# The gate of an attention block worked out before the attention: alpha on the softmax output, one minus alpha on the recurrence's queries

## The reference

```
n = layernorm(x);  q, k, v = split(n @ Wqkv + b)
y_soft = softmax(q k^T / 4 + causal mask) @ v
state_t = retention * state_(t-1) + Gamma * (v_t outer k_t / 4);  y_stp_t = (W_static + state_t) @ q_t
alpha = sigmoid(gelu(n @ gate_w1 + gate_b1) @ gate_w2 + gate_b2)      one value per row and head
x = x + (alpha * y_soft + (1 - alpha) * y_stp) @ out_w + out_b
x = x + ffn(layernorm(x))       matmul in fp8, one scale from the largest |value| of all rows
```

## Time and profile before

| what | value |
|---|---|
| median of 3 runs | 1819.63 us (1816.71 to 1822.33) |
| the profiled execution | 1821.89 us, span 1820.2 us |
| PE, DVE, ACT, POOL busy over the span | 91%, 84%, 76%, 65% |
| mean granted TensorE clock | 0.944 |
| DMA, mean | 90 GB/s |

### The profile page before, as it was taken

The page is one execution under the profiler, slowest core; times in us unless marked ns, Lnnn a source line. Parts: engine busy times, 40 slices in busy tenths (PEclk is TensorE's granted clock), DMA queues, the critical chain, the costliest instruction groups (busy, mean ns, idle before and its releaser), DMA issues. The chain is left out here.

```text
span 1820.2 us, 44569 instructions
## 1 busy us (share of the span) xinstructions
PE 1653.8 (91%) x17464; PEld 597.0 (33%) x17464; DVE 1521.2 (84%) x1717; ACT 1391.2 (76%) x2835; POOL 1187.7 (65%) x1138
## 2 busy tenths in 40 slices
PE   4898589999999999999999999999999999996745
PEld 2553113332333333323333333333333233332632
DVE  3556889999989999998899999989999999811777
ACT  1453158889888888898888988998889989985333
POOL 1100568777777777787777777877788889840720
PEclk9898569999999999999999999999999999998865
DMA  2685441223122422231224232321243121101602
GB/s 80 216 259 168 114 101 62 85 64 99 59 68 84 111 65 82 68 95 59 71 82 111 66 87 73 87 78 63 85 117 89 50 94 48 57 10 50 230 19 81
DMA packets 115345, 163.19 MB, mean 90 GB/s; under 512 B 30081, under 2 KB 57793, under 8 KB 115137
## 3 DMA queue, kind: packets, MB, share of 16 engines
q1 hardware_dynamic: 112608, 158.74, 29.6%
q10 hardware_dynamic: 2528, 1.64, 0.3%
HBM read 121.87 MB, written 38.01 MB: 88 GB/s over the span
## 5 line engine op out<-in xcount | busy, mean ns | idle before, releaser
L1420 DVE TENSOR_REDUCE pmax<-PS 128x2 f32<-128x1024 f32 (+2 forms) x1120 | 1204.4, 1129 | 87.3 <-PE PS L1221 66.1
L1373 ACT ACTIVATE probs<-PS 128x512 f32<-128x512 f32 (+3 forms) x2304 | 1150.8, 573 | 165.0 <-PE PS L1259 82.9
L1284 PE MATMUL PS<-probs,V_g 128*17 128x256 f32 (+3 forms) x5064 | 398.5, 387 | 11.1 <-ACT o_t L1394 10.7
L1129 POOL TENSOR_TENSOR v_exp<-v_exp,k_rows 128x512 f32<-128x512 f32 x256 | 321.6, 1283 | 24.9 <-DMA v_exp<-qkv_t 24.7
L1259 PE MATMUL PS<-Q_st,K_st 50*128 50x512 f16 (+3 forms) x1408 | 287.4, 366 | 7.6 <-ACT probs L1373 6.5
L1171 POOL TENSOR_TENSOR state<-odd,q_rows 128x514 f32<-128x514 f32 x256 | 281.8, 1132 | 6.1
L1221 PE MATMUL PS<-K_st,Q_st 48*128 48x512 f16 (+3 forms) x1408 | 272.7, 357 | 0.2
L1284 PE MATMUL PS<-probs,V_first 128*17 128x256 f32 (+2 forms) x3296 | 265.5, 394 | 2.2 <-ACT o_t L1394 2.2
L1259 PE MATMUL PS<-Q_st,K_first 50*128 50x512 f16 (+3 forms) x896 | 194.3, 380 | 11.4 <-ACT probs L1373 5.4
L1221 PE MATMUL PS<-K_first,Q_st 48*128 48x512 f16 (+1 forms) x832 | 179.2, 393 | 18.8 <-DVE pmax L1420 18.5
L1160 POOL COPY carry<-odd 128x4 f32<-128x4 f32 x64 | 12.0, 187 | 259.7 <-DVE odd L1455 259.7
(11 more groups left out here) (170 smaller groups left out, 1475.1 us busy)
## 6 DMA issues: line engine op xcount, KB each, us to landing
v_exp<-qkv_t SPq DMA_DIRECT2D x256, 256.0 KB
qkv_t<-proj SPq DMA_DIRECT2D x24, 512.0 KB, 3.8
qk_parts<-parts SPq DMA_DIRECT2D x16, 512.0 KB, 5.3
Q_st<-qk_parts SPq DMA_DIRECT2D x192, 32.0 KB, 3.7
v_rows<-vaug SPq DMA_DIRECT2D x8, 544.0 KB, 6.1
xin<-x SPq DMA_DIRECT2D x8, 512.0 KB, 6.3
k_rows<-qkv_t SPq DMA_DIRECT2D x16, 256.0 KB, 4.1
q_rows<-qkv_t SPq DMA_DIRECT2D x16, 256.0 KB, 6.1
```

What stands on the lines that cost most here:

```text
L1129: pool.tensor_tensor(v_exp[:, n % RING], v_exp[:, n % RING], k_rows[:, b % 2], ALU.mult)\
L1284: mm = pe.matmul(PS[h * VW:h * VW + VN, O_BANK, first:end], v[:, kt, h * VN:(h + 1) * VN], probs[:, tile % P_SLOTS, h, first - r * P:end - ...
L1373: act.activation(probs[:, tile % P_SLOTS, h, 0:CH - r * P], PS[:, step[5], 0:CH - r * P], ACT.Exp, scale=SCORE_SCALE).then_inc(exp_done, 1)
L1420: dve.tensor_reduce(pmax[:, s % 2, pair * TPC + j:GH * TPC:PAIRS * TPC, blk], PS[:, bank:bank + SIDES, 0:width], AX.X, ALU.max).then_inc(m ...
```

## The change

alpha is worked out at the end of the prologue, in place in `z`: POOL adds the bias and, after ACT's exp, the one; DVE takes the reciprocal between two row maxima (`GATE_AT` = 16 pairs taken). PE turns it to heads on partitions, ACT makes beta = 1 - alpha from that, and SP stores it (`beta_t`, 16 heads by 4096 rows). In the attention `out_norm` multiplies the reciprocal of the sums by alpha (one more DVE instruction, 128x16), and `load_kq` loads beta too, each head's row onto its 16 partitions; POOL multiplies `q_rows` by it ahead of `lag_products_of`. All of the recurrence's output is linear in q, so what is stored is (1 - alpha) y_stp. The last block turns the softmax to channels and adds the two there; it has no rows-to-channels copy, no alpha and one DVE instruction of 128x1024 in the place of four of 128x512. The gate's logits are made for rows in their natural order now.

```
@@ prologue, SP
+                    sp.wait_ge(beta_made, 1)
+                    for n in range(TPC):
+                        sp.dma_start(beta_t[:, n * (T // TPC):(n + 1) * (T // TPC)].rearrange("h (a p) -> a h p", p=P),
+                                     beta[:, n, :]).then_inc(beta_stored, 16)
@@ prologue, POOL, at its end
+                    pool.wait_ge(z_evac, NCH + 1)
+                    pool.tensor_tensor(z[:, :, :], z[:, :, :], b2_sb[:, :].unsqueeze(1).broadcast_to([P, NT, H]), ALU.add)\
+                        .then_inc(logits_biased, 1)
+                    pool.wait_ge(gate_exp, 1)
+                    pool.tensor_tensor(z[:, :, :], z[:, :, :], ones[:, 0:1].unsqueeze(1).broadcast_to([P, NT, H]), ALU.add)\
+                        .then_inc(gate_sum, 1)
@@ prologue, PE turn_back
-                            mm = pe.matmul(PS[:, PROJ_BANK + 1, j * H:(j + 1) * H], gate_t[:, par, slice(j // 2 * PAIR + j % 2, (j // 2 + 1) * PAIR, 2)],
+                            mm = pe.matmul(PS[:, PROJ_BANK + 1, j * H:(j + 1) * H], gate_t[:, par, j * P:(j + 1) * P],
@@ prologue, PE, between the last first_maxima
+                        if pairs_made == GATE_AT + 2:
+                            pe.wait_ge(gate_ready, 1)
...
+                                mm = pe.transpose(PS[:, PROJ_BANK, n * P:(n + 1) * P],
...
+                            mm.then_inc(gate_turned, 1)
@@ prologue, ACT, at its end
+                    act.wait_ge(logits_biased, 1)
+                    act.activation(z[:, :, :], z[:, :, :], ACT.Exp, scale=-1.0).then_inc(gate_exp, 1)
+                    act.wait_ge(gate_turned, 1)
+                    act.activation(beta[:, :, :].rearrange("p n t -> p (n t)"), PS[:, PROJ_BANK, :], ACT.Identity,
+                                   bias=ones[:, 0:1], scale=-1.0).then_inc(beta_made, 1)
@@ prologue, DVE, between the last first_maxima
+                        if pairs_taken == GATE_AT:
+                            dve.wait_ge(gate_sum, 1)
+                            dve.reciprocal(z[:, :, :], z[:, :, :]).then_inc(gate_ready, 1)
@@ attention, SP load_kq, between the loads of q_rows and v_chan
+                        sp.dma_start(beta_rows[:, :], beta_t[half * HPH:(half + 1) * HPH, cols].unsqueeze(1)
+                                     .broadcast_to([HPH, HD, CH])).then_inc(beta_loaded, 16)
@@ attention, POOL lag_products_of (kq is now the first half of beta_rows)
+                        pool.wait_ge(beta_loaded, (g * N_SWEEPS + b + 1) * 16)
+                        pool.tensor_tensor(q_rows[:, b % 2, 1:1 + CH], q_rows[:, b % 2, 1:1 + CH], beta_rows[:, :], ALU.mult)\
+                            .then_inc(q_weighed, 1)
+                        pool.wait_ge(q_weighed, g * N_SWEEPS + b + 1)
@@ attention, DVE out_norm, between reciprocal and product
+                                dve.tensor_tensor(rden[:, s % 2], rden[:, s % 2],
+                                                  z[:, TPC * ORDER[s]:TPC * (ORDER[s] + 1), g * GH:(g + 1) * GH], ALU.mult)\
+                                    .then_inc(denom_gated, 1)
+                                dve.wait_ge(denom_gated, g * NCH + s + 1)
@@ last block, SP (waits soft_turned for soft, y_added for stp)
-                            sp.dma_start(stp[:, par], y_stp_t[:, :, bass.ds(it * (2 * CH) + par * CH + PAD, CH)]
-                                         .rearrange("f p t -> p f t")).then_inc(soft_loaded[par], 16)
+                            for half in range(HALF):
+                                sp.dma_start(stp[:, par, half, :],
+                                             y_stp_t[half, :, bass.ds(it * (2 * CH) + par * CH + PAD, CH)]
+                                             .rearrange("(i h) t -> h i t", h=HPH)).then_inc(stp_loaded[par], 16)
@@ last block: the stages of the first pipeline
-                    pipeline(pool, (1, residual), (0, weigh), (2, power))
+                    pipeline(pool, (0, residual), (1, power))
-                    pipeline(pe, (0, turn_stp), (2, project), (1, turn_y))
+                    pipeline(pe, (0, turn_soft), (1, project))
-                    pipeline(act, (1, columns), (2, normalise))
+                    pipeline(act, (0, normalise))
-                    pipeline(dve, (1, merge), (0, difference), (2, add_attention), (3, largest))
+                    def add_recurrence(it, par):
+                        dve.wait_ge(soft_turned, it * 2 + par + 3)
+                        dve.wait_ge(stp_loaded[par], it * 32 + 32)
+                        dve.wait_ge(attn_ready, it * 2 + par + 1)
+                        dve.tensor_tensor(y_t[:, par], PS[:, 2 * par:2 * par + 2, :], stp[:, par], ALU.add).then_inc(y_added, 1)
+                    pipeline(dve, (0, add_recurrence), (1, add_attention), (2, largest))
```

More of the change, by code:

```diff
@@ L476, in preln_attention_ffn_kernel @@
             ones = sb("ones", [P, 2], where=pro)
+            beta = sb("beta", [P, TPC, P], where=pro)
             bounds = sb("bounds", [P, 4], where=pro)
@@ L977, in preln_attention_ffn_kernel @@
             v_chan = sb("v_chan", [P, CH], where=att)
+            beta_rows = sb("beta_rows", [P, CH], where=att)
             v_exp = sb("v_exp", [P, RING, CH], where=att)
@@ L1292, in lag @@
                         pe.wait_ge(lag_products, g * N_SWEEPS + b + 1)
-                        pe.matmul(PS[:, bank, 0:PAIR], lag_sum[:, b % HALF, :], kq[:, :], start=True, stop=True)\
+                        pe.matmul(PS[:, bank, 0:PAIR], lag_sum[:, b % HALF, :], beta_rows[:, 0:PAIR], start=True, stop=True)\
                             .then_inc(lag_ready, 1)
@@ L1473, in preln_attention_ffn_kernel @@
             xn2 = sb("xn2", [P, NT, D], where=fin)
-            alpha = sb("alpha", [P, NT, H], where=fin)
             soft = sb("soft", [P, 2, TPC, D], where=fin)
@@ L1478, in preln_attention_ffn_kernel @@
             xb = sb("xb", [P, 2, TPC, D], where=fin)
-            diff = sb("diff", [P, 2, TPC, D], where=fin)
-            y = sb("y", [P, 2, TPC, D], where=fin)
             y_t = sb("y_t", [P, 2, HALF, CH], where=fin)
@@ L1585, in _ @@
                 def _(pe):
-                    def turn_stp(it, par):
-                        pe.wait_ge(soft_loaded[par], it * LOADS_PER_CHUNK + LOADS_PER_CHUNK)
-                        pe.wait_ge(y_made, it * 2 + par + 1)
-                        for half in range(HALF):
-                            for j in range(TPC):
-                                mm = pe.transpose(PS[:, 2 * par + half, j * P:(j + 1) * P],
-                                                  stp[:, par, half, j % 2 * PAIR + j // 2 * P:j % 2 * PAIR + (j // 2 + 1) * P],
-                                                  ident[:, :])
-                        mm.then_inc(stp_turned, 1)
@@ L1655, in _ @@
                 def _(act):
-                    def columns(it, par):
-                        act.wait_ge(y_turned, it * 2 + par + 1)
-                        act.wait_ge(attn_ready, it * 2 + par + 1)
-                        for c in range(HALF):
-                            act.activation(y_t[:, par, c, :], PS[:, 4 + c, :], ACT.Identity).then_inc(yt_evac, 1)
                     def normalise(it, par):
@@ L1671, in normalise @@
                         ins.then_inc(xn2_made, 1)
-                    act.wait_ge(gate_chain, 1)
-                    act.activation(alpha[:, :, :], z[:, :, :], ACT.Exp, scale=-1.0).then_inc(gate_exp, 1)
-                    pipeline(act, (1, columns), (2, normalise))
+                    pipeline(act, (0, normalise))
                     def rounded_columns(it, par):
@@ L1698, in _ @@
                 def _(dve):
[L1699 to L1722 removed]
+                    def add_recurrence(it, par):
+                        dve.wait_ge(soft_turned, it * 2 + par + 3)
+                        dve.wait_ge(stp_loaded[par], it * 32 + 32)
+                        dve.wait_ge(attn_ready, it * 2 + par + 1)
+                        dve.sem_inc(beats, 1)
+                        dve.tensor_tensor(y_t[:, par], PS[:, 2 * par:2 * par + 2, :], stp[:, par], ALU.add).then_inc(y_added, 1)
                     def add_attention(it, par):
```

82 lines of the change are left out of this document (31 added, 51 removed).

## The result

The changed kernel takes 1841.93 us (median of 4 runs, 1841.21 to 1844.04) beside 1820.98 us for the kernel before (4 runs, 1816.71 to 1825.87): a ratio of 1.0127, 95% interval 1.0108 to 1.0147 (the medians alone give 1.0115). It is slower by 1.2 to 1.3%, some 21 to 23 us, and outside the range that was given. The profiled execution has a span of 1839.0 us, against 1820.2 before.

The account below looks back on a forecast made before the run. PE's list, DVE close behind, was taken to set the pace. 3.35 + 1.3 + 3.0 + 2.0 - 11.3 + 0.2 = -1.45 us gave 1820.4 profiled, 1818.2 as median; range 1811 to 1827.

Parts of the forecast that it names:

- Gate in the prologue, +3.35: Prologue's end: DVE's reciprocal of 128x512 does not hide in its gapless row of maxima, +3.35 us; block ends at 193.5.
- First q times beta, +1.3: Attention's start: POOL's new product ahead of the first lag_products_of goes through to PE and DVE, +1.3 us.
- alpha in out_norm, +3.0 (0 to 9): Attention, 32 times: one more DVE instruction of 128x16, 0.20 us each with its wait, pushing PE some 3 us in all.
- The step's other half: Attention's out_norms: each added delay pushes PE by 0.26 us minus its distance, 0.8 us a group, some 3 for four.
- q times beta in the other 15 sweeps, +2.0 (0 to 4): Attention's later sweeps: POOL's extra 1.3 us fits its idle time, but five to eight more scans run slowed, +2.0 us.
- The last block, -11.3 (-12.5 to -5): Last block: first x1 sum 6.4 us earlier, seven steps at 5.96 us save 4.9, together -11.3 us.
- the even race between loads and DVE: Last block: loads take 6.1 us a chunk beside DVE's 5.96; DVE was taken as the bound.
- its rival of half the DMA engines: Last block: loads at 152 GB/s take 6.9 us a chunk and bound the steps; +5.0, 1824.6 us, chance 0.12.
- POOL passing its product on: Attention: POOL's 1.3 us reaches scan and PE in each of 15 sweeps, 19.5 us; +16, 1835.7 us, chance 0.14.
- The test that the text set itself: Prediction wrong on the whole if the attention is longer by more than 10 us, or by none.
- The faster rival: PE makes up the cost of out_norm and scans, last block gives its 12.5; -7.9, 1811.8 us, chance 0.22.
- the one of the clock: Last block: PE stays at 1.2 GHz, 6.4 to 6.8 us a step; 1821.3 us, chance within the forecast's 0.52.

Follow-up runs that it names:

- t_noprod: Changed kernel without the gate product (times alpha) in out_norm: 1818.86 us, ratio 0.9998 to the kernel before.
- t_spread: Changed kernel with the last block's stp read by one plain DMA a chunk, the attention's store already in head order: 1834.08 us, ratio 1.0093 to the kernel before.
- t_seventh: Changed kernel without the gate product in the seventh out_norm of each group, the other 28 kept: 1831.51 us, ratio 1.0058 to the kernel before.
- t_psum: Changed kernel with z kept at 1/alpha, denominators multiplied by it straight from PSUM, then the reciprocal: 1823.47 us, ratio 1.0029 to the kernel before.
- t_loadonly: Changed kernel without the out_norm gate product and without POOL's q times beta, beta's load kept: 1817.17 us, ratio 0.9995 to the kernel before.
- experiment 3: The run of t_psum: changed kernel with the out_norm product taken from PSUM before the reciprocal, 1823.47 us, ratio 1.0029 to the kernel before.
- experiment 2: Changed kernel without q times beta on POOL and without beta's load, gate product in out_norm kept: 1832.26 us, ratio 1.0081 to the kernel before.

## Why the prediction failed

*Gate in the prologue, +3.35: right, though the block did not end at 193.5.* It ended at 190.4. DVE's row in the changed kernel,

```profile
162.83 6.62 DVE L978 TENSOR_REDUCE pmax<-PS 128x2 f32<-128x1024 f32 x6 [2.83 <-PE PS L680]
169.36 3.34 DVE L998 RECIPROCAL z<-z 128x512 f32<-128x512 f32 x1
172.61 3.75 DVE L978 TENSOR_REDUCE pmax<-PS 128x2 f32<-128x1024 f32 x4
```

is longer by the reciprocal and starts 3.4 us sooner, because PE had a higher granted clock between 45 and 60 us. The window in the profile of before (length, busy of PE, PEclk, DMA share, GB/s):

```profile
45.00:60.00 15.00, 10.23 (x32) 0.66 0.73 246
```

and in the changed kernel's:

```profile
45.00:60.00 15.00, 11.02 (x41) 0.89 0.74 249
```

That varies from execution to execution: `t_noprod`, `t_spread` and `t_seventh` had 0.66 there, and their attention starts at 194.0, 193.7 and 193.3, 3 us behind the 190.6 of before at the same 0.66; `t_psum` and `t_loadonly` had 0.89, and start at 189.8 and 190.7 like the changed kernel.

*First q times beta, +1.3: right.* PE stood 3.40 us (3.3 was said), DVE 4.02 instead of 2.67.

*alpha in out_norm, +3.0 (0 to 9): the step that failed.* It cost 21.7 us by the traces, 23 by the medians. The price of the instruction was read from one tiny product at 1758 us, where POOL was idle, and carried to places where POOL works. The step's other half was sound: the way in which a delay passes to PE, counted place by place, gives 3.5 us when the product is 0.16 us long (experiment 3). In its place stand a hold-up until the end of POOL's instruction, up to 1.25 us, passed on to PE almost one to one, and at the turns of the groups the fall of the clock. The three add up to the 20.9 us behind the out_norms: 3.5 for the step, 12.1 for what the 32 products take over 0.17 us each, and 5.4 for the two falls.
The profile of before held the warning, and the prediction used it one step further on: DVE's scan, with two inputs in SBUF, took 2.23 us beside POOL and not 1.22. I priced this for eight scans and did not ask which other instruction has that form; the one that the change adds 32 times does. The Trainium skill says it outright: by "SBUF — State Buffer" (Who interferes with whom) a DVE instruction with two SBUF inputs contends with a GpSimd instruction that reads SBUF, as its second input comes through the read interface that the two engines share, and by the same page (Summary: rules for kernel authors) the one that issues second is blocked until the first has finished. By that rule any of the 32 products that begins beside POOL's 1.25 us product waits for its rest; the traces of the changed kernel and of experiment 3 agree, with 0.17 to 1.25 us for the form from SBUF and 0.164 us on average for the form from PSUM.

*q times beta in the other 15 sweeps, +2.0 (0 to 4): not refuted.* With the product in out_norm away, the attention is longer by 7.0 us with it and the load than without (1492.0 and 1485.0), 1.5 of them at the start. But of these two profiles one is the slowest of its twelve executions and the other is below its median; the ratios, 0.9998 and 0.9984, differ by 2.5 us for start and sweeps together. The stretches behind scans say the same: against the kernel before they hold 0.1 to 5.6 us more in the eight kernels that have this product, 3.0 on average, and -1.4 to 0.3 in the three that have not. Fewer scans were slowed than forecast: 6 of 64 over 1.8 us in the changed kernel, where 9 to 12 were said (9 are over 1.5, against 4 before). What the forecast had not seen is that the product moved POOL's instructions to where they met the out_norms three times more (experiment 2).

*The last block, -11.3 (-12.5 to -5): right in kind, -8.8 by the traces.* The first x1 sum came 17.7 us after the block's start (17 was said), the last 60.8 (59). The start gave 5.1 us where 6.4 were said, since DVE's first two sums waited 11.8 and 5.3 us for `stp`, and the seven steps 3.5 where 4.9 were said: 6.15 us each, not 5.96. Of the even race between loads and DVE I took the wrong winner. The prediction's own 6.1 us a chunk for the loads is about what was measured (5.91 to 6.51 in seven profiles); its rival of half the DMA engines had the kind right, and was too high with 6.9. DVE alone was put too high as well: with the plain load the step is 5.67.

*Rivals.* The one that ends above, POOL passing its product on, came near the time (1835.7) by the wrong way: no wait of PE for POOL stands in the attention except the 3.40 us at its start, and without the products of DVE the time was back at 1818.9. The test that the text set itself, an attention longer by more than 10 us, was met with 27.8. The faster rival, in which the attention hides it all, is refuted by the same number, and the one of the clock by the last block's windows, with a granted clock of 1.00 from 1726 us on.

## What to carry to other kernels

A small instruction on the way between two engines is priced at the place where it goes, with what the other engines do there: look for an instruction of the same form, with its operands in the same memories, that runs beside the same neighbour. A DVE instruction with two SBUF inputs beside a busy POOL can wait for all of POOL's running instruction, up to 1.25 us here; give it one input in PSUM where the arithmetic can be turned round, here by keeping 1/alpha. And what stops PE a little longer at a place where it already stops costs more than its length, since the clock may fall behind it.

## What the hardware showed that was not expected

- The hold-up is as long as what remains of POOL's instruction, so a shift of POOL's row by a fraction of a microsecond decides between 0.2 and 1.1 us at the same place (0.22, 0.58 and 1.12 in three kernels).
- A fall of PE's clock at a turn cost 2.0 and 3.4 us beyond the hold-up itself. It came behind 6 of 9 stops of some 2.2 us, the first and the third turn in each of the three profiles, and behind 1 of 27 stops of 1.05 to 1.26 us.
- POOL's power took 82 us for 128x512; DVE's reciprocal took 3.34 us, and ACT's logarithm and exponential 0.63 us each with a table load of 1.28 us before either.
